# Attention in a one-layer vision transformer: softmax sums by TensorE, and the division on the outputs

## The reference, cut to what matters

```python
h = h + attention(layernorm(h)) @ w_o
h = h + ffn(layernorm(h))

def attention(x):
    q, k, v = split(x @ w_qkv)
    q, k = rope(q), rope(k)
    scores = einsum('bhqd,bhkd->bhqk', q, k) * 16 ** -0.5 + causal_bias
    attn = softmax(scores, axis=-1)
    return einsum('bhqk,bhkd->bhqd', attn, v)
```

## Time and profile before

| what | us |
|---|---|
| median of 3 runs (286.29 to 287.82) | 287.52 |
| the profiled execution | 288.25 |
| its span | 286.5 |
| TensorE busy | 251.3 |
| VectorE busy | 180.9 |
| ScalarE busy | 57.3 |
| POOL busy | 47.3 |

### The profile page before, as it was taken

The page is one execution under the profiler, slowest core; times in us unless marked ns, Lnnn a source line. Parts: engine busy times, 40 slices in busy tenths (PEclk is TensorE's granted clock), DMA queues, the critical chain, the costliest instruction groups (busy, mean ns, idle before and its releaser), DMA issues.

```text
span 286.5 us, 4830 instructions
## 1 busy us (share of the span) xinstructions
PE 251.3 (88%) x1956; PEld 206.0 (72%) x1956; DVE 180.9 (63%) x461; ACT 57.3 (20%) x104; POOL 47.3 (17%) x65
## 2 busy tenths in 40 slices
PE   3995199588866689999999989989989999999996
PEld 2563167367755348888988989978868888888764
DVE  0005518978677642999999999889995867522100
ACT  1100000834334314222412273400000000000000
POOL 4002312700211152222504252000000000000000
PEclk9998569999997569999999999999999999999999
DMA  7950000013000036206113460030000000000000
GB/s 259 383 191 0 0 2 0 1 46 105 24 26 21 22 93 201 74 1 201 58 37 94 135 196 21 0 87 0 2 0 18 2 18 2 0 18 2 18 0 11
DMA packets 14805, 16.99 MB, mean 59 GB/s; under 512 B 848, under 2 KB 12992, under 8 KB 14784
## 3 DMA queue, kind: packets, MB, share of 16 engines
q1 hardware_dynamic: 13776, 15.70, 16.9%
q10 hardware_dynamic: 1008, 1.00, 1.0%
HBM read 15.48 MB, written 1.21 MB: 58 GB/s over the span
## 4 chain that ended last, share of the span: by engine, by line
PE 50%; DVE 38%; issue 4%; POOL 3%; ACT 2%; DMA 1%; DVEq 0%
PE ps L1018 22%; PE ps L981 9%; PE ps L792 6%; PE ps L1040 5%; DVE topi L666 3%; DVE big L765 3%; PE ps L805 3%; DVE top L663 3%; PE ps L1015 2%; PE ps L937 2%; POOL rs L326 2%; DVE big L524 2%; DVE stats L494 2%; DVE red L566 2%; DVE big L580 2%
## 5 line engine op out<-in xcount | busy, mean ns | idle before, releaser
L1018 PE MATMUL ps<-ue,big 128*128 128x256 f32 (+1 forms) x320 | 72.3, 381 | 1.4 <-DVE big L765 1.4
L1018 PEld LDWEIGHTS ps<-ue,big 128*128 128x128 f32 (+1 forms) x320 | 57.3, 182 | 12.0 <-DVE big L765 1.8
L981 PE MATMUL ps<-hn_hi,de_hi 128*128 128x296 f32 x128 | 40.7, 318 | 2.0 <-ACT big L466 1.1
L765 DVE TENSOR_TENSOR big<-ps,big 128x1024 f32<-128x1024 f32 (+1 forms) x19 | 22.7, 1197 | 26.9 <-PE ps L1040 26.2
L981 PE MATMUL ps<-hn_lo,de_hi 128*128 128x296 f32 x128 | 38.4, 300 | 0.0
L981 PE MATMUL ps<-hn_hi,de_lo 128*128 128x296 f32 x128 | 38.2, 299 | 0.0
L466 ACT ACTIVATE big<-ps 128x592 f32<-128x592 f32 x32 | 21.1, 665 | 44.5 <-PE ps L981 44.4
L981 PEld LDWEIGHTS ps<-hn_hi,de_hi 128*128 128x128 f32 x128 | 24.1, 188 | 4.5 <-DVE actT L712 1.9
L981 PEld LDWEIGHTS ps<-hn_lo,de_hi 128*128 128x128 f32 x128 | 24.1, 188 | 1.2 <-issue 1.2
L981 PEld LDWEIGHTS ps<-hn_hi,de_lo 128*128 128x128 f32 x128 | 24.1, 189 | 0.0
L792 PE MATMUL ps<-big 128*111 128x256 f32 (+1 forms) x72 | 20.1, 431 | 4.5 <-DMA big<-in_w_tok 4.5
(11 more groups left out here) (113 smaller groups left out, 345.7 us busy)
## 6 DMA issues: line engine op xcount, KB each, us to landing
de<-in_down_t SPq DMA_DIRECT2D x16, 256.0 KB, 2.8
ue<-in_up_e SPq DMA_DIRECT2D x4, 1024.0 KB, 6.1
big<-in_patches SPq DMA_DIRECT2D x6, 296.0 KB, 5.2
big<-in_w_tok ACTq DMA_DIRECT2D x6, 128.0 KB, 5.4
big<-in_w_qkv SPq DMA_DIRECT2D x1, 768.0 KB, 8.7
h_scratch<-big SPq DMA_DIRECT2D x5, 111.0 KB
late<-in_keys_bd SPq DMA_DIRECT2D x1, 512.0 KB, 9.8
downT<-in_wdown_t SPq DMA_DIRECT2D x1, 512.0 KB, 9.2
```

Of the source, the lines that this page charges most:

```text
L765: chain(nc.vector.tensor_tensor(dst, pv, dst, ALU.mult), g_ready)
L981: last = mm(ps[:, 2 + 2 * (e % 2) + a, 0:HALF], half[:, (e // 2) % SPLITS, k, own], src[:, k, a * HALF:(a + 1) * HALF], start=(n == 0), st ...
L1018: last = mm(acc, sil[:, e, j * 128:j * 128 + Q * v], ue[:, e, :], start=False, stop=(e == EX - 1))
```

## The change

The exponentials are no longer divided. TensorE transposes them as they are, and eight more matmuls in `attend` multiply the transposed exponentials with the 0/1 constant, which gives each head's sum, repeated over the head's 16 rows, in the free half of bank 7. VectorE takes the reciprocal of these sums (a new tile `rden`) and multiplies it with the attention outputs of bank 6 into `oT`, in `normalise(gi)`. ScalarE's copy of oT is gone, and its exponentials stand ahead of hn_copy. softmax_back is gone, and VectorE's queue is written out anew.

```diff
-                act.wait_ge(pe_o, gi + 1)
-                if gi >= 2:
-                    act.wait_ge(pe_wo, gi - 1)
-                nc.scalar.copy(oT[:, gi % 2, :, 0:r],
-                               ps[:, 6, 0:256].rearrange("p (a r) -> p a r", a=2)[:, :, 0:r]).then_inc(oT_ready, 1)
+                if gi + 2 < NG:
+                    exponentials(gi + 2)
                 if gi >= NG - 2:
                     gated_copy(2 * (gi - NG + 2) + 1)
                 if gi >= 1:
                     hn_copy(gi - 1)
-                if gi + 2 < NG:
-                    exponentials(gi + 2)
...
-            def softmax_back(gi):
...
+            def normalise(gi):
                 r = GROUPS[gi][1] * S
+                dve.wait_ge(pe_o, gi + 1)
+                if gi >= 2:
+                    dve.wait_ge(pe_wo, gi - 1)
+                behind()
+                chain(nc.vector.reciprocal(rden[:, :, 0:r], side_by_side(7, 256, r)))
+                behind()
+                chain(nc.vector.tensor_tensor(oT[:, gi % 2, :, 0:r], side_by_side(6, 0, r), rden[:, :, 0:r], ALU.mult),
+                      oT_ready)
...
-            softmax_back(0)
             values(6)
             softmax_front(1)
-            for gi in range(1, NG):
-                softmax_back(gi)
-                if gi + 1 < NG:
-                    softmax_front(gi + 1)
-                else:
-                    gated_rest(0)
-                    gated_rest(1)
-                hidden(gi - 1)
+            for gi in range(NG):
+                if gi + 2 < NG:
+                    softmax_front(gi + 2)
+                normalise(gi)
+                if gi >= NG - 2:
+                    gated_rest(gi - NG + 2)
+                if gi >= 1:
+                    hidden(gi - 1)
             hidden(NG - 1)
...
             def probs_T(gi):
                 r = GROUPS[gi][1] * S
-                pe.wait_ge(prob_ready, gi + 1)
+                pe.wait_ge(exp_done, gi + 1)
...
             def attend(gi):
...
+                r = n * S
+                for c in range(PAIRS):
+                    p0 = 32 * (c % 4)
+                    col = 256 + 128 * (c // 4)
+                    last = mm(ps[p0:p0 + 32, 7, col:col + r], con[0:2 * S, C_PAR:C_PAR + 2 * DK],
+                              pT[0:2 * S, gi % 2, c, 0:r], start=True, stop=True, tile_position=(0, p0))
                 last.then_inc(pe_o, 1)
```

More of the change, by code:

```diff
@@ L185, in vit_tower @@
         veps, nhalf = sb("veps", [128, 1]), sb("nhalf", [128, 1])
-        red = sb("red", [128, 3, H])
+        red = sb("red", [128, 1, H])
+        rden = sb("rden", [128, 2, ROWS])
         top = sb("top", [128, 2, FH, TOPK])
@@ L216, in flat, with side_by_side @@
             return ps[:, bank:bank + 2, :].rearrange("p a c -> p (a c)")[:, 0:width]
+        def side_by_side(bank, col, r):
+            return ps[:, bank, col:col + 256].rearrange("p (a r) -> p a r", a=2)[:, :, 0:r]
         def halves(tile):
@@ L240, in vit_tower @@
         pe_vT, vT_ready, pe_v, v_dve, v_act = sem("pe_vT"), sem("vT_ready"), sem("pe_v"), sem("v_dve"), sem("v_act")
-        pe_sc, sc_sub, exp_done, prob_ready = sem("pe_sc"), sem("sc_sub"), sem("exp_done"), sem("prob_ready")
+        pe_sc, sc_sub, exp_done = sem("pe_sc"), sem("sc_sub"), sem("exp_done")
         pe_pT, pT_ready, pe_o, oT_ready, pe_wo = (
@@ L570, in softmax_front @@
                                               .broadcast_to([r, RT, HR, S]), ALU.subtract), sc_sub)
-            def softmax_back(gi):
+            def normalise(gi):
                 r = GROUPS[gi][1] * S
-                dve.wait_ge(exp_done, gi + 1)
+                dve.wait_ge(pe_o, gi + 1)
+                if gi >= 2:
+                    dve.wait_ge(pe_wo, gi - 1)
                 behind()
-                chain(nc.vector.tensor_reduce(red[0:r, 1, :], pr[0:r, gi % 2], AX.X, ALU.add))
+                chain(nc.vector.reciprocal(rden[:, :, 0:r], side_by_side(7, 256, r)))
                 behind()
[L578 to L582, removed]
+                chain(nc.vector.tensor_tensor(oT[:, gi % 2, :, 0:r], side_by_side(6, 0, r), rden[:, :, 0:r], ALU.mult),
+                      oT_ready)
             def hidden(gi):
```

## The result

The change makes the kernel **slower: 312.62 us** (median of 4 runs, 311.94 to 313.30) against 287.62 of the kernel before (286.29 to 287.82, 4 runs beside it), a ratio of 1.087 [1.083, 1.092]. The profiled execution of after took 312.09 us with a span of 310.3, 23.8 over the span of before.

The account below looks back on a forecast made before the run. VectorE was taken to bound the attention stage; engines taking turns add 18.0 us, the clock 5.7 in bursts and 3.0 in last pieces, 26.7 in all: 288.25 + 26.7 - 0.73 = 314.2, stated as 314.0 us, range 303 to 325.

Parts of the forecast that it names:

- What bounds the kernel before: In the attention over six groups, VectorE's chain bounds at 6.30 us a period; TensorE runs about half a period ahead.
- The reciprocal: VectorE's reciprocal of 222 elements in normalise, 1.54 us from the slope of two short rows; ends 0.39 and 3.5.
- The rival of a slow reciprocal: Eight cycles an element in normalise's reciprocal, 316.7 us, or 324 at the far end; chance 0.13.
- The product: VectorE's product of 222 elements out of PSUM in normalise, 0.39 us, priced by hidden's add.
- The sums: Eight added TensorE matmuls per group, 0.64 us, beside softmax_front and on the path only for the last two groups.
- The turns: In the attention, VectorE and TensorE wait for each other: 9.8 us a full period against 6.30, queries 18.0 us later.
- The clock: TensorE's granted clock falls in its waits within the attention stage: 5.7 us in bursts plus 3.0 in last pieces.
- each long burst: TensorE's work up to scores(3), scores(4) and scores(5), each losing 1.9 us at the lower clock, 5.7 in all.
- the last pieces: rows_T and probs_T(4), attend(4) and sums, and rows_T(3), wholly at half speed: 3.0 us more.
- Clock kept high: Same loop of turns, but TensorE's clock never falls, nor at the queries: 303.6 us; chance 0.12.
- Clock low throughout: Every TensorE piece on the path runs at half speed, and up to 1.9 us more at the queries: about 320; chance 0.10.
- only VectorE's load counts: Scores ready in time, normalise simply takes softmax_back's place: 287 to 289 us, or 283 with a low-end reciprocal; chance 0.06.

Follow-up runs that it names:

- experiment 8: Kernel before the change, hidden split, next softmax_back filling the rstd wait, exponentials ahead of hn_copy: 282.54 and 282.71 us, or 286.55 to 288.01 us.
- experiment 7: Kernel before the change, hidden split, softmax_front(gi + 1) or gated_rest filling the rstd wait, hidden's add thereby ahead of softmax_front: 296.73 us.
- experiment 4: Changed kernel, reciprocal of only the first 8 columns of each half, one column serving the whole product: 304.35 us.
- Experiment 5: Changed kernel without the eight sum matmuls of each group, the reciprocal reading what attend wrote: 310.33 us.
- experiment 3: Changed kernel with idle matmuls in TensorE's waits, five ahead of project and two ahead of rows_T: 304.31 us.
- experiment 6: Changed kernel with TensorE's next transposes, scores and attend ahead of its waits for VectorE, and hidden split with softmax_front or gated_rest in the gap: 291.37 us.
- experiment 10: Idle matmuls ahead of the clock's fall, in the kernel of experiment 8 (281.33 us) and the kernel before (284.95 to 286.37, or 290.19 and 290.25 us).
- experiment 9: Three idle matmuls ahead of the last rows_T, on experiment 8 (282.01 to 282.76, or 287.60 to 288.31 us) and on the kernel before (290.00 us).
- e13_before_idle: Kernel before the change with idle matmuls ahead of the clock's fall: 284.95 to 286.37 us in four executions, 290.19 and 290.25 in two.
- e2_fill: The run of experiment 3: changed kernel with idle matmuls ahead of project and rows_T, 304.31 us.
- e12_gap_back_idle: Kernel of experiment 8 with idle matmuls ahead of project, attend(4), attend(5) and the last rows_T: 281.33 us.
- e11_before_fill: Kernel before the change with three idle matmuls ahead of the last rows_T: 290.00 us.
- e9_gap_back: The run of experiment 8: kernel before the change, softmax_back filling the rstd wait, 282.54 and 282.71 us, or 286.55 to 288.01 us.
- e6_mended: The run of experiment 6: changed kernel with mended queue order and hidden split in two, 291.37 us.

## Why the prediction was right

314.0 us was forecast with a range of 303 to 325, and 312.62 was measured. Step by step:

- *What bounds the kernel before*: VectorE, with TensorE half a period ahead. Experiments 8 and 7 bear it out from two sides: a shorter turn of VectorE makes a shorter period (5.42 us), and TensorE's lead lost makes a longer one (7.2 to 9.2 us).
- *The reciprocal.* 1.54 us forecast from the slope of two short rows, 1.547 measured; over 16, 74 and 222 elements (253, 621, 1547 ns) it is 6.3 ns an element throughout, and the same 16 elements took 258 ns out of PSUM (experiment 4), where the 253 ns were out of SBUF. The rule of the Trainium skill (VectorE: DVE Perf Modes, "Walkthrough: the 8-slice pipeline in each mode") with its repeat count of 8 made an estimate of 2.0 us, and the trace does not agree. The rival of a slow reciprocal falls with it. The product: 0.39 forecast, 389 ns measured.
- *The sums.* 0.64 us, beside softmax_front. This is a term that was mis-sized: for attend(4) and its sums I counted 1.28 us and doubled it for the clock, 2.56, and the chain has 1.04 us (107.57 to 108.61). A quarter of a microsecond of this is overlap, since most sums run beside the end of attend. The rest is the clock: I had it at its lower level there, and it was granted at 1.00 from 107.5 to 108.7 us. Experiment 5 puts the sums' net part in the stage at 0.2 us, between two profiles.
- *The turns.* At full clock the forecast was 55.4 us from the first maximum to the queries (64.40 to 119.8); experiment 3, at full clock, shows 54.62 (63.12 to 117.74). One full turn: 9.8 forecast, 9.55 there; the short one 8.7 forecast, 8.61 there.
- *The clock.* 8.7 us forecast in the stage; 62.00 - 54.62 = 7.4 measured. The step behind it was rougher than its sum: I had each long burst lose 1.9 us. The first, from project to the end of scores, took 6.57 us (70.29 to 76.86) against 3.86 at full clock, 2.7 lost. Against experiment 3 the three turns lost 2.7, 1.3 and 1.7 us and the last pieces 1.7, where 1.9, 1.9, 1.9 and 3.0 were forecast; the errors partly cancel, which is luck. Nor did I expect the queries to get worse, which they did by 0.99.
- *The sum.* 26.7 us forecast, 23.8 between the two profiled executions: 2.1 too much in the stage (64.1 against 62.0, of which the attend and sums named above are 1.5), 0.99 too little in the queries, and 1.71 by which this execution reached the stage earlier, all but 0.09 of which the change did not do. That 314.0 lies within 1.4 us of the median owes something to this: the stage was forecast too long and the queries too short.
- *The rivals.* Clock kept high, 303.6 us: made by experiment 3, it comes to 304.31, though its queries still took 6.12 us, where the rival had them 1.9 shorter than before; a shorter stage makes up for part of it. Clock low throughout, about 320: it was granted at 1.00 from 88 to 92 us. That only VectorE's load counts was to be decided by whether the maximum over group 3 starts right behind normalise(0): that ends at 70.24 and the maximum starts at 76.88.

What stays open: whether the change's arithmetic in the order of experiment 6, with idle matmuls as in experiment 10, would come below 287 us. It was not tried. Why some executions of experiments 8 and 9 kept the clock without help is not shown either; only that the time goes with it. Nor is it shown why two of the six executions of e13_before_idle took 290.2 us, with a mean granted clock of 0.959 against 0.970 to 0.976 in the other four; neither of the two was profiled.

## What to carry to other kernels

Before moving work from one engine to another, write down for both queues, side by side, which instruction each wait needs, and what stands ahead of that: as long as one engine's next input does not stand behind something that waits for the other's last output, they overlap; if it does, their times add up, whatever the busy times say. Price the order before the arithmetic: here the arithmetic was worth nothing either way on VectorE's load, and mending the order 17.9 us. And where TensorE waits in a stage, look at its granted clock there and in what follows; idle matmuls in its waits paid for themselves in two kernels where they stood ahead of the fall, and cost time behind it. In the kernel before they paid in four executions of six only, so look at all executions and not at the median.

## What the runs showed of the hardware

- Work that nobody reads made a kernel faster twice, by 8.3 us (e2_fill) and by about 6 against the slower of the two times of experiment 8 (e12_gap_back_idle). In e13_before_idle four executions were faster by about 1.8 us and two slower by about 2.4. Put behind the fall of the clock, it cost 2.3 us (e11_before_fill).
- One and the same kernel showed two times 5 us apart, with a mean granted clock of 0.963 and about 0.943 (e9_gap_back), and with idle matmuls in TensorE's waits six executions showed one (e12_gap_back_idle). It is no rule: the kernel before, 285.98 to 288.80 us in all its executions, took 284.95 to 286.37 us in four executions with such matmuls and 290.2 us in two (e13_before_idle).
- The queries, the same 16 records, took 7.41, 6.42 and 4.55 us in three kernels (after, before, e12_gap_back_idle), at a mean granted clock of 0.61, 0.70 and 1.00.
- POOL's reciprocal root (L331) took 0.57 us in general, but 0.85 us in e6_mended in the three places where VectorE's gated_rest ran beside it:

```profile
88.43 0.57 POOL L331 TENSOR_TENSOR rs<-veps,nhalf 111x1 f32<-111x1 f32 x1
...
94.27 0.85 POOL L331 TENSOR_TENSOR rs<-veps,nhalf 111x1 f32<-111x1 f32 x1
```
